# Gated decay attention: scores from rounded high and low parts of rotated queries and keys

## The reference, cut to what matters

```python
q = _apply_rope(q, cos, sin)
k = _apply_rope(k, cos, sin)
...
scores = jnp.einsum('bhnid,bhnjd->bhnij', qc, kc)
decay = jnp.where(causal, jnp.exp(G[..., :, None] - G[..., None, :]), 0.0)
y_intra = jnp.einsum('bhnij,bhnjd->bhnid', scores * decay, xc)
...
y = y / rms * gnorm_w
gate = (hidden_states @ Wg.T).reshape(B, L, H, D)
y = y * (gate * jax.nn.sigmoid(gate))
return y.reshape(B, L, H * D) @ Wo.T
```

## Time and profile before

| | |
|---|---|
| runs | 1470.19, 1472.35, 1472.77 us; median 1472.35 |
| profiled execution | 1467.15 us |
| its span in the profile | 1465.0 us |
| mean granted clock of TensorE | 0.991 of full speed |
| TensorE, VectorE, ScalarE, GpSimd busy in the span | 1407.8, 1090.4, 854.6, 604.5 us |

### The profile page before, as it was taken

One profiled execution on the slowest core, in us unless ns is written; L12 is line 12 of the kernel. 1 busy time (PEld: TensorE's weight loads), 2 busy tenths in 40 slices (PEclk: granted clock), 3 DMA queues, 4 the chain that ended last, 5 costly groups with the idle time before them and its releaser, 6 DMA issues.

```text
span 1465.0 us, 24269 instructions
## 1 busy us (share of the span) xinstructions
PE 1407.8 (96%) x7610; PEld 1167.8 (80%) x7610; DVE 1090.4 (74%) x2485; ACT 854.6 (58%) x2146; POOL 604.5 (41%) x633
## 2 busy tenths in 40 slices
PE   7999999999989989999999999879999999999997
PEld 6788888887778867787778778668888888888873
DVE  5697667697688877767776776767788788788884
ACT  4556555655223157656755755648677677677660
POOL 4555444444022137556655745435243243242110
PEclk9999999999999999999999999999999999999999
DMA  8011110102122341330321321310111022012000
GB/s 323 1 73 72 73 63 9 72 33 102 58 87 87 114 135 55 103 128 30 130 100 47 111 101 58 129 73 30 40 63 73 15 73 86 15 72 78 1 0 29
DMA packets 30133, 107.72 MB, mean 74 GB/s; under 512 B 3847, under 2 KB 13191, under 8 KB 22104
## 3 DMA queue, kind: packets, MB, share of 16 engines
q1 hardware_dynamic: 30040, 106.58, 20.1%
HBM read 97.07 MB, written 9.50 MB: 73 GB/s over the span
## 4 chain that ended last, share of the span: by engine, by line
PE 53%; DVE 17%; issue 16%; POOL 8%; ACT 4%; DMA 1%; POOLq 0%; DVEq 0%; SPq 0%; ACTq 0%
PE bank L186 11%; PE bank L187 10%; PE bank L188 10%; PE bank L1774 3%; POOL yss L1407 2%; PE bank L316 2%; PE bank L1789 2%; PE bank L339 2%; PE bank L1795 2%; PE bank L1791 2%; POOL tmp L159 1%; PE bank L1231 1%; PE bank L1732 1%; PE bank L327 1%; PE bank L285 1%
## 5 line engine op out<-in xcount | busy, mean ns | idle before, releaser
L159 POOL TENSOR_TENSOR tmp<-tmp,sin 128x512 f32<-128x512 f32 x80 | 111.5, 1394 | 211.2 <-ACT tmp L152 211.2
L188 PE MATMUL bank<-wo_low,att_high 128*128 128x512 f32 x384 | 150.7, 392 | 0.0
L2073 DVE SCALAR_TENSOR_TENSOR logit<-bank,qss,amask 128x512 f32<-128x512 f32 x128 | 90.9, 747 | 57.0 <-PE bank L188 55.9
L1986 POOL TENSOR_TENSOR qss<-qss,half 128x4 f32<-128x4 f32 x32 | 34.9, 1090 | 199.6 <-DVE qss L2059 199.6
L1607 PE MATMUL bank<-kT,wg 128*128 128x256 f32 x512 | 113.1, 383 | 4.0 <-ACT prob L1641 4.0
L1893 ACT ACTIVATE prob<-logit,rmax 128x512 f32<-128x512 f32 x128 | 91.6, 719 | 37.8 <-DVE rmax L2077 37.8
L1607 PEld LDWEIGHTS bank<-kT,wg 128*128 128x128 f32 x512 | 98.1, 192 | 17.9 <-ACT prob L1641 4.4
L186 PE MATMUL bank<-l_wo_high,att_high 128*128 128x512 f32 x256 | 104.7, 409 | 1.8 <-DVE att_low L1491 1.1
L187 PE MATMUL bank<-xT_high,wq_low 128*128 128x512 f32 x256 | 102.3, 400 | 0.0
L187 PE MATMUL bank<-l_wo_high,att_low 128*128 128x512 f32 x256 | 99.8, 390 | 0.0
L1907 ACT ACTIVATE p_high<-bank 128x512 fp32r<-128x512 f32 x128 | 70.1, 597 | 46.4 <-PE bank L1774 46.1
(11 more groups left out here) (270 smaller groups left out, 4414.1 us busy)
## 6 DMA issues: line engine op xcount, KB each, us to landing
wq<-in_l_wq SPq DMA_DIRECT2D x16, 1024.0 KB, 6.6
wo<-in_l_wo SPq DMA_DIRECT2D x16, 1024.0 KB, 5.0
wkv<-in_l_wkv SPq DMA_DIRECT2D x16, 512.0 KB, 5.7
wg<-in_l_wg SPq DMA_DIRECT2D x8, 1024.0 KB, 4.8
wq<-in_x_wq SPq DMA_DIRECT2D x8, 1024.0 KB, 7.2
wo<-in_x_wo SPq DMA_DIRECT2D x8, 1024.0 KB, 4.9
kT<-in_x_wkv SPq DMA_DIRECT2D x8, 512.0 KB, 4.2
kv_keys<-logit SPq DMA_DIRECT2D x8, 512.0 KB, 4.6
```

What stands on the lines that cost most here:

```text
L159: eng.tensor_tensor(halves(tmp[4 + j % 2]), halves(tmp[2 + j % 2]), per_batch(sin), ALU.mult).then_inc(sem(f"{l}_sinp"), 1)
L188: return eng.matmul(dst, a_high, b_low, start=False, stop=stop)
L2073: dve.scalar_tensor_tensor(logit[s % 2][:, c, :], bank[3 + c][:, :], qss[p][:, 1, h, 2 * b + c:2 * b + c + 1], amask[:, c, :], ALU.mult, A ...
```

## The change

Each rotated head is now summed in place, into `tmp[j % 2]`. ScalarE rounds this into a high part (`l1_round`), and VectorE subtracts the high part from the sum to give the low part (`l1_rounded_rest`). High and low parts lie where `qT` and `kT` lay; they have one buffer for all groups, where the old tiles had two, so the rounding waits for the last group's scores. A score is then three fp32r products. The copy-outs of this stage wait for the low part of head j-2 (`l1_low`) instead of its sum (`l1_rope`). Some semaphores elsewhere are merged into one with a doubled count (`sink_in` and `sink_sum` into `sink_vector`, `sink_exp` and `sink_ln` into `sink_scalar`, `dt_turn` into `dt`).

```diff
             if due(5 * g + j - 1):
-                eng.wait_ge(sem(f"{l}_rope"), 5 * g + j - 1)
+                eng.wait_ge(sem("l0_rope" if l == "l0" else "l1_low"), 5 * g + j - 1)
...
+        l1_q = [over("l1_q_high", [P, GH, T], "qT0"), over("l1_q_low", [P, GH, T], "qT1")]
+        l1_k = [over("l1_k_high", [P, T], "kT0"), over("l1_k_low", [P, T], "kT1")]
+
+        def l1_part(i, j):
+            return l1_k[i][:, :] if j == 0 else l1_q[i][:, j - 1, :]
+
+        def l1_round(act, g, j):
+            act.wait_ge(sem("l1_rope"), 5 * g + j + 1)
+            if due(6 * g):
+                act.wait_ge(sem("l1_score"), 6 * g)
+            act.activation(l1_part(0, j), tmp[j % 2][:, :], ACT.Copy).then_inc(sem("l1_high"), 1)
+
+        def l1_rounded_rest(dve, g, j):
+            dve.wait_ge(sem("l1_high"), 5 * g + j + 1)
+            dve.tensor_tensor(l1_part(1, j), tmp[j % 2][:, :], l1_part(0, j).bitcast(F32), ALU.subtract)\
+               .then_inc(sem("l1_low"), 1)
...
                             if m == 0:
-                                pe.wait_ge(sem("l1_rope"), 5 * g + 5)
+                                pe.wait_ge(sem("l1_low"), 5 * g + 5)
...
-                        pe.matmul(bank[3 + m][:, :], kT[p][:, b * L + kt * P:b * L + (kt + 1) * P],
-                                  qT[p][:, :, b * L + qt * P:b * L + (qt + 1) * P], start=True, stop=True)\
-                          .then_inc(sem("l1_score"), 1)
+                        product(pe, bank[3 + m][:, :],
+                                [k[:, b * L + kt * P:b * L + (kt + 1) * P] for k in l1_k],
+                                [q[:, :, b * L + qt * P:b * L + (qt + 1) * P] for q in l1_q], True, True)\
+                            .then_inc(sem("l1_score"), 1)
...
-                for j in range(GH):
-                    rope_psum_copies(act, "l1", g, j + 1, bank[(j + 1) % 2])
+                for j in range(1, GH + 1):
+                    rope_psum_copies(act, "l1", g, j, bank[j % 2])
+                    if j > 1:
+                        l1_round(act, g, j - 1)
                 decays(0)
+                l1_round(act, g, GH)
                 decays(1)
...
                 headed(1)
+                if not last_group:
+                    l1_round(act, n, 0)
                 squares(3)
...
             value(0, 0, bank[4])
-            act.wait_ge(sem("dt_turn"), 1)
+            l1_round(act, 0, 0)
+            act.wait_ge(sem("dt"), 2)
...
-                rope_sum(dve, "l1", g, 1, qT[p][:, 0, :])
+                rope_sum(dve, "l1", g, 1, tmp[1][:, :])
                 exponents(1, 0)
-                rope_sum(dve, "l1", g, 2, qT[p][:, 1, :])
+                rope_sum(dve, "l1", g, 2, tmp[0][:, :])
+                l1_rounded_rest(dve, g, 1)
                 exponents(1, 1)
-                rope_sum(dve, "l1", g, 3, qT[p][:, 2, :])
-                rope_sum(dve, "l1", g, 4, qT[p][:, 3, :])
+                rope_sum(dve, "l1", g, 3, tmp[1][:, :])
+                l1_rounded_rest(dve, g, 2)
+                rope_sum(dve, "l1", g, 4, tmp[0][:, :])
+                l1_rounded_rest(dve, g, 3)
+                l1_rounded_rest(dve, g, 4)
...
-                    rope_sum(dve, "l1", n, 0, kT[1 - p][:, 0:T])
+                    rope_sum(dve, "l1", n, 0, tmp[0][:, :])
                 gated(2)
+                if not last_group:
+                    l1_rounded_rest(dve, n, 0)
...
-            rope_sum(dve, "l1", 0, 0, kT[0][:, 0:T])
+            rope_sum(dve, "l1", 0, 0, tmp[0][:, :])
+            l1_rounded_rest(dve, 0, 0)
```

More of the change, by code:

```diff
@@ L845, in mix_vector @@
                 step(dve, dve.tensor_reduce(vec4(mx), lines, AX.X, ALU.max))
-                dve.tensor_tensor(t4, src, wide(mx), ALU.subtract).then_inc(sem("sink_in"), 1)
-                dve.wait_ge(sem("sink_exp"), side + 1)
+                dve.tensor_tensor(t4, src, wide(mx), ALU.subtract).then_inc(sem("sink_vector"), 1)
+                dve.wait_ge(sem("sink_scalar"), 2 * side + 1)
                 t_lines = t4 if side == 0 else rows4(ztmp[:, :, :], True)
-                dve.tensor_reduce(vec4(zsm[:, 2, :]), t_lines, AX.X, ALU.add).then_inc(sem("sink_sum"), 1)
-                dve.wait_ge(sem("sink_ln"), side + 1)
+                dve.tensor_reduce(vec4(zsm[:, 2, :]), t_lines, AX.X, ALU.add).then_inc(sem("sink_vector"), 1)
+                dve.wait_ge(sem("sink_scalar"), 2 * side + 2)
                 step(dve, dve.tensor_tensor(ls, ls, mx, ALU.add))
@@ L975, in sink_scalar @@
             for side in range(2):
[L976 to L979, removed]
+                act.wait_ge(sem("sink_vector"), 2 * side + 1)
+                act.activation(z, z, ACT.Exp).then_inc(sem("sink_scalar"), 1)
+                act.wait_ge(sem("sink_vector"), 2 * side + 2)
+                act.activation(zsm[:, 1, :], zsm[:, 2, :], ACT.Ln).then_inc(sem("sink_scalar"), 1)
             act.wait_ge(sem("mix_ready"), 1)
@@ L1083, in dt_turn @@
                 last = pe.transpose(bank[5][:, n * 32:(n + 1) * 32], src[:, at:at + P], ident[0:32, 0:32])
-            last.then_inc(sem("dt_turn"), 1)
+            last.then_inc(sem("dt"), 1)
         def dt_scalar(act):
@@ L1502, in body @@
                 exponents(0, 1)
-                if due(6 * (g - 1)):
-                    dve.wait_ge(sem("l1_score"), 6 * (g - 1))
-                rope_sum(dve, "l1", g, 1, qT[p][:, 0, :])
+                rope_sum(dve, "l1", g, 1, tmp[1][:, :])
                 exponents(1, 0)
-                rope_sum(dve, "l1", g, 2, qT[p][:, 1, :])
+                rope_sum(dve, "l1", g, 2, tmp[0][:, :])
+                l1_rounded_rest(dve, g, 1)
                 exponents(1, 1)
-                rope_sum(dve, "l1", g, 3, qT[p][:, 2, :])
-                rope_sum(dve, "l1", g, 4, qT[p][:, 3, :])
+                rope_sum(dve, "l1", g, 3, tmp[1][:, :])
[3 more added lines that the diff above has]
+                l1_rounded_rest(dve, g, 4)
                 clamp(0)
@@ L1526, in body @@
                 if not last_group:
-                    if due(6 * g):
-                        dve.wait_ge(sem("l1_score"), 6 * g)
-                    rope_sum(dve, "l1", n, 0, kT[1 - p][:, 0:T])
+                    rope_sum(dve, "l1", n, 0, tmp[0][:, :])
                 gated(2)
+                if not last_group:
+                    l1_rounded_rest(dve, n, 0)
                 mean(3)
```

## The result

The changed kernel takes 1522.95 us (median of 4 runs, 1521.12 to 1524.34), the one before 1471.27 us beside it: 3.5% slower, ratio 1.035 with a 95% interval of 1.033 to 1.037. The difference is 51.7 us where 44 were forecast, and the time lies in the forecast range of 1500 to 1534. The profiled execution took 1524.34 us.

The account below looks back on a forecast made before the run. TensorE, busy 52.40 of 53 us a group, was taken to set the stage. Losses of 7.5 (first group), 6 x 5.3 and 4.7 (last) sum to 44 us on the 1472.35 median: 1516 us, range 1500 to 1534.

Parts of the forecast that it names:

- Release of tmp: Before gates(0): query 3's copy-out waits for query 1's subtraction on VectorE, leaving TensorE idle 2.4 us.
- the next copy-out: Before gates(1): query 4's copy-out waits for query 2's subtraction, making gates(1) another 2.4 us late.
- the last head: Before the scores: last sum, rounding and subtractions of queries 3 and 4 start scores 5.85 us late in all.
- Scores, TensorE: Score products: nine rounded products replace three exact ones, saving 1.16 us a group, 9.3 us in all, if nothing waits.
- Rest of the group: After the scores: ScalarE's extra 1.3 us lateness is absorbed; last transposes wait 0.65 longer; a steady group costs 5.3 us.
- likeliest case: Whole kernel: 1516 us, reaching from 1505 (shorter latencies at three waits a group) to 1528 (slower product); chance 0.68.
- the slower product: Scores: a rounded product whose operand steps over heads might exceed the assumed 0.23 us, giving the upper bound of 1528.
- The clock: TensorE's clock in the gated decay attention: the sum takes no loss from it falling after the new waits.
- rival C: Gated decay attention: the new 2.4 us waits also cost TensorE clock, 1543 us, or 1530 with half hidden; chance 0.15.
- A: Copy-outs and last head: subtractions come early enough, nothing is held back, 9.3 us saved, 1463 us; chance 0.04.
- B: Copy-outs stay on time, only the last head's tail counts, about 2.2 us a group, 1490 us; chance 0.10.
- Load: New work on VectorE and ScalarE: 3 us more each per group fits, costing nothing through load, only through its place.

Follow-up runs that it names:

- e1: Changed kernel with rotated sums written where the low part lies, so copy-outs wait for the sum again: 1515.55 us, ratio 1.031.
- e3: Kernel before with scores as three products of high parts only, sums rounded as written, no low parts, roundings or subtractions: 1466.43 us, ratio 0.997.
- e2: Changed kernel with the next key's rounding behind squares(3) and its subtraction behind mean(3): 1519.43 us, ratio 1.033.
- e9: e1 with first-sequence scores begun with the products needing only the fourth query's high part: 1499.88 us, ratio 1.020.
- e7: e1 and e2 together, plus second-sequence exponents behind weights(0) and their exponentials behind sigmoid(1): 1489.42 us, ratio 1.012.
- e8: e5 with first-sequence products needing no low query part first, and the next key's rounding behind the gate weights': 1463.87 us, ratio 0.995.
- e6: Control: kernel before, exact scores, no new roundings, with e5's moves of exponents, exponentials, squares, means, powers and gated product: 1459.47 us, ratio 0.991.
- e5: e7 with the late chain reordered (squares, means, powers, gated product earlier) and group 0's key rounding behind the first copy-out: 1470.03 us, ratio 1.000.

## Why the prediction was right, and where it was off

*The direction and its cause.* Right, and shown. "The copy-out of head j now waits for the subtraction of head j-2" was the step the forecast rested on: ScalarE's waits of 3.42 and 2.71 us name the subtraction, and e1 takes them away with the release alone.

*Release of tmp, the next copy-out, the last head.* 2.4, 2.4 and 5.85 us in all were forecast; start to start it is 2.4, 2.4 and 6.04 in all (where the slowed gates fill part of such a gap, the wait shown is shorter, the start the same). The 0.2 more at the last head is the two subtractions, 1.69 us together beside GpSimd's products.

*Scores, TensorE.* 1.16 us a group forecast, 0.97 measured, in the change as in e3. That the saving "counts in full" holds for no kernel that keeps the old order: e3 gets 0.4.

*Rest of the group.* This is the step that failed in size. "The difference of 1.3 is less than the 1.89 us that ScalarE waits for the last gate, so it is absorbed" looked at one waiter. ScalarE's lateness against TensorE also reaches outputs(1, 1), through GpSimd's subtractions, the powers and the gated products, and there the slack was 0.15 us: the wait costs 0.6. GpSimd ends these subtractions 1.1 us behind TensorE's start on the next key before the change and 1.8 behind it in the changed kernel. They are 1.8 behind in e3 as well, which has no new work on ScalarE: what is handed back here is the products' saving. The added wait before the last transposes was put at 0.65, all of it for the key's rounding ahead of squares(3), and came to 0.9; e2 returned 0.5 of it, and the rest has no cause shown.

The working for a steady group becomes 6.04 - 0.97 + 0.6 + 0.9 = 6.6, against 6.5 measured and 5.3 forecast. Group 0 lost 7.8 (forecast 7.5): the second copy of the decay columns comes at 601.20 instead of 591.23, of which 2.2 had come in before the changed work: ScalarE copies the first values at 539.88 instead of 537.68, and in the traces of e1 to e9 this copy lies anywhere from 537.5 to 539.4. The six steady groups lost 39.0 (forecast 31.8). With 5 for the last group (4.7 forecast) that is 52 us, the difference of the medians. The profiled executions differ by 57.2: to the changed one come those 2.2 us and 3.5 us more lost to the clock from the last group on (0.86 over 50 us where it was 0.93), in code that the change does not touch.

*The bounds.* Two terms of the likeliest case, 1505 to 1528, do not hold. Two latencies of 0.3 at three waits are 1.8 us a group, not 1.4, and give 1502. For the slower product behind the 1528 there is no row and no run: nine products took 2.16 us in the change, 0.24 each. The range of 1500 to 1534 does not hang on either.

*The clock.* The forecast took no loss and gave a chance of 0.15 to one that hits every group (rival C). The clock did fall in every steady group, so what it said would make it wrong did happen, but the time did not follow: the fall lay in gates that had to wait anyway, as the forecast argued for gates(0). In e1 and e9 it lies in the open and costs its 1.7 and 1.2 us. The Trainium skill, "TensorE: Matmul & The Clock Gate", section on HAM oscillation, tells of a loop whose wait for a DMA, longer than the waits of the change, brings the lower clock back in every iteration. The traces agree for the waits of 3.4 us in e1; in the change waits of 2.1 to 2.3 did the same, in e9 waits of 2.3 to 2.4 did it in every second group, and at 1.3 and 1.6 us (e7) no steady group has it.

*Rivals A and B.* A (subtractions early enough) never came true by itself. e8 comes to 1463.9, where A stood at 1463, but by coincidence: it holds the moves that are worth 11 us on the exact kernel (e6), and TensorE still waits 0.35 and 0.65 us by turns for the last rounding. B (copy-outs on time, only the tail of the last head counts, 1490) is e1's edit, which came to 1515: it had left out VectorE's delays ahead of the last head and the clock.

*Load.* Right in part. 3 us more on VectorE and on ScalarE cost 51.7 us net of the cheaper products in one order, 10.6 in a second (e5 against e6) and 4.4 in a third (e8 against e6, which has the split products in an order that exact ones cannot have). "It costs through its place" holds for most of it; that it costs nothing in the best order is not shown.

## What to carry to other kernels

A cheaper product on the engine that sets the time is worth its saving only if the operands it needs are ready as early as before; follow the buffer that the new step holds, and who waits for it, before counting the saving. When a chain grows late, look at everything it releases and take the one with the least slack, not the one with the longest wait. Try the order alone as a control: here reordering the old kernel gave 11 us, more than the 7.8 us (0.97 a group) that the new products could give at best.

## What the runs showed of the hardware

- In these runs a fall of TensorE's clock had a price only where TensorE had no wait behind it to be filled. With one fall in each group, the change lost next to nothing by it (59.5 to 59.6 us whether it fell into gates(0) or gates(1)), e1 1.7 us a group and e9 1.2 us in each second one. Removing two waits of 2.1 to 2.3 us ahead of another brought it into the open.
- In e9 the same loop fell into two kinds of iteration that take turns, 57.1 and 55.9 us, with and without the fall. One iteration of such a loop is not enough to read its cost from.
- A tiny VectorE operation can take seven times as long: the mean of 128x4 takes 0.15 us, and 1.01 when it starts beside GpSimd's 128x512 subtractions for the query weights (e3 and the change). It ends when GpSimd's operation does: at 756.71 against 756.67 in the change, at 726.32 against 726.29 in e3.
